# Last phase of a four-layer graph network: reciprocals taken per node, the self term applied while the fourth layer drains, statistics and output by round

## The chip, the cores and the metric

The kernel runs on one core of one Trainium2 chip. The metric is device time in microseconds, the median of several runs; less is better. Engines are named as in the profile: PE multiplies matrices (PEld is its weight load), DVE works elementwise, ACT is ScalarE, POOL is GpSimd, SP issues DMAs.

## What is computed

Node features `x` of 3125 nodes by 64 pass four pre-normalised residual layers over 53125 edges (50000 in both directions and a self loop for each node), which are sorted by destination. The change lies at the end of the fourth:

```python
h = jnp.maximum(_layernorm(x, axis=-1), 0.0)
...
attn = jnp.einsum('ehd,ehd->eh', q[edge_src], k)
amax = jax.ops.segment_max(attn, edge_src, num_segments=n)
ex = jnp.exp(attn - amax[edge_src])
denom = jax.ops.segment_sum(ex, edge_src, num_segments=n)
alpha = ex / (denom[edge_src] + 1e-16)
upd = jax.ops.segment_sum(v * alpha[..., None], edge_src, num_segments=n)
upd = upd.reshape(n, OV) @ W_out
out = tfn_features @ W_self + upd
mu = out.mean(axis=0)
var = out.var(axis=0)
return (out - mu) * jax.lax.rsqrt(var + EPS_BN) * gamma + beta
```

Here `tfn_features` is `h`; there are 8 heads of 16 columns (`OV` = 128), `W_out` is 128 by 64, `W_self` 64 by 64, and the result is added to `x`. Mean and variance run over the nodes, for each of the 64 columns.

## The kernel before

The fourth layer runs over 416 tiles of 128 edges, in groups of four tiles (`GT`), eight groups (`UG`) to a loop iteration, 13 iterations (`NI`), all written out. It is a pipeline of steps: at step (i, k) a group's node rows are transposed, the group before it is multiplied on PE (`products`), the one before that is turned into keys and values on DVE (`keys_and_values`), and so on. `lag(i, k, n)` gives the group that is n steps behind, or nothing. The last stages are `values` (DVE: value rows times softmax weight into the two-deep buffer `M3`), a step later `sums` on PE (per tile one f32 product for the values, L1915, and one bf16 product for the denominators, L1916) in two halves of two tiles, and `add_sums` on DVE, which scales one column of the running sum `acc` (L2087) and adds the tile's sums (L2092). A half of the sums must be there before its adds, and its bank is free again only after them. Every `KG` = 4 groups a softmax step runs through all engines; p1 and p2 in the bodies are its two parts.

After the last group has entered, iteration i == NI has eight more steps, the drain, in which only the later stages have work: no gathers, no `products` but one group, and two halves of softmax. What is in order on an engine there is fixed by the functions `body`, one for each engine.

`acc[:, 0]` then holds, transposed, 128 value columns for each node, and rows 0 to 23 of `acc[:, 1]` hold the denominators, in three parts of 8 heads that must be added. Node n = 25 p + j stands at column n; `node_cols` gives the 125 nodes of one j as a strided view (`NJ` = 25, `PN` = 125). `HT` is `h` transposed, 64 by 3125, column block j for the 125 nodes of j. `rounds(NJ, 4)`, also called `R3`, has six rounds of four blocks (500 columns) and one of one block.

The last phase is a block of its own (L2145 to L2230), behind a barrier of the engines. For each round PE multiplies the 24 rows by `sel_b`, a matrix of zeros and ones that adds the three parts and repeats a head over its 16 columns (L2189; rows 8 to 23 of `sel_b` are copied by two DMAs on SP at the phase's start, L2224); DVE adds 1e-16, takes reciprocals of 128 by 500 and multiplies `acc` in place (L2162, L2163, L2165); PE adds `W_self` and `W_out` products in one bank (L2199, L2200); ACT copies the result to `OT` and adds up its columns (L2214). Then come the mean, one squaring pass over 3125 columns on ACT (L2217), the root (L2219, with a load of its function table), the normalisation of the whole in one DVE instruction (L2176), transposes back on PE (L2206), the add to `X` (L2179) and seven DMAs to the output (L2228).

Of the kernel before, what the change touches and what calls it, by code (L numbers as in the profile page):

```python
# [26 lines left out]
ALU = mybir.AluOpType  # L27
ACT = mybir.ActivationFunctionType
AX = mybir.AxisListType

N = 3125
# [61 lines left out]
def build(nc, A, out):  # L93
    with ExitStack() as ctx:
# [1598 lines left out]
        bcol = sb("bcol", [D, 1])  # L1693
        sel_b = sb("sel_b", [24, 128])
# [45 lines left out]
        fac_cols = bank[7][:, 416:448]  # L1740
        kv_of = lambda k: psum[:, (2 + k % 2 * 2) * 512:(4 + k % 2 * 2) * 512].rearrange("p (t f) -> p t f", t=GT)
# [19 lines left out]
        with nc.Block() as block:  # L1761
            @block.gpsimd
            def _(pool):
                def queries(g):
                    if g >= QR:
                        pool.wait_ge(e3_ev, (g - QR + 1) * 2)
                    for t in range(GT):
# [3 lines left out]
                n = 0  # L1771
                pool.memset(sel_b[0:8, :], 1.0).then_inc(n3_p, 1)
                n += 1
                pool.wait_ge(n3_p, n)

                pool.affine_select(out=sel_b[0:8, :], in_=sel_b[0:8, :], compare_op=ALU.is_ge, fill=0.0, base=0,
                                   pattern=[[1, 128]], channel_multiplier=-16).then_inc(n3_p, 1)
                n += 1
                pool.wait_ge(n3_p, n)
                pool.affine_select(out=sel_b[0:8, :], in_=sel_b[0:8, :], compare_op=ALU.is_ge, fill=0.0, base=15,  # L1780
                                   pattern=[[-1, 128]], channel_multiplier=16).then_inc(n3_p, 1)
# [17 lines left out]
            def _(sp):  # L1799
# [104 lines left out]
            def _(pe):  # L1904
# [34 lines left out]
                def body(i, k):  # L1939
# [9 lines left out]
                    for t in range(GT):  # L1949
# [33 lines left out]

                for r, (j0, n) in enumerate(R3):
# [13 lines left out]
                pe.wait_ge(n3_p, 4)  # L1998
# [4 lines left out]
            def _(dve):  # L2003
# [102 lines left out]
                def body(i, k):  # L2106
# [31 lines left out]
                    if val:  # L2138
                        values(*val)
# [5 lines left out]
        m3_r, m3_b, m3_u, m3_m, m3_c, m3_dve, m3_sd, m3_t, m3_x, m3_o, m3_s = [sem("m3_" + x) for x in  # L2145
            ("r", "b", "u", "m", "c", "dve", "sd", "t", "x", "o", "s")]
        OT = tmp("OT", [D, N])
        OC = tmp("OC", [D, N])
        sq = tmp("sq", [D, N])
        osum = tmp("osum", [D, 8])  # L2150
        rden = tmp("rden", [128, 2, 512])
        bn = tmp("bn", [D, 8])
        CH = rounds(NJ, 4)
        m3_q = sem("m3_q")
        with nc.Block() as block:  # L2155
            @block.vector
            def _(dve):
                c = Chain(dve, m3_r)
                for n, (a, w) in enumerate(CH):
                    dve.wait_ge(m3_b, n + 1)  # L2160
                    r = rden[:, n % 2, 0:w * PN]
                    c.link(dve.tensor_scalar(r, bank[n % 2][:, 0:w * PN], 1e-16, None, ALU.add))  # L2162
                    c.link(dve.reciprocal(r, r))  # L2163
                    v = node_cols(acc[:, 0])[:, a:a + w, :]
                    dve.tensor_tensor(v, v, r.rearrange("c (j p) -> c j p", j=w), ALU.mult).then_inc(m3_u, 1)  # L2165
                dve.wait_ge(m3_c, len(CH))
                c = Chain(dve, m3_dve)
                c.link(dve.tensor_reduce(bn[:, 0:1], osum[:, 0:len(CH)], AX.X, ALU.add))
                c.link(dve.tensor_scalar(bn[:, 1:2], bn[:, 0:1], -1.0 / N, None, ALU.mult))
                c.link(dve.tensor_scalar(OC[:], OT[:], bn[:, 1:2], None, ALU.add))  # L2170
                dve.wait_ge(m3_q, 1)
                c.link(dve.tensor_scalar(bn[:, 3:4], bn[:, 2:3], 1.0 / N, EPS, ALU.mult, ALU.add))
                dve.wait_ge(m3_sd, 1)
                c.link(dve.reciprocal(bn[:, 5:6], bn[:, 4:5]))
                c.link(dve.tensor_tensor(bn[:, 6:7], bn[:, 5:6], gcol[:], ALU.mult))
                c.link(dve.tensor_scalar(OT[:], OC[:], bn[:, 6:7], bcol[:, 0:1], ALU.mult, ALU.add))  # L2176
                for r, (j0, n) in enumerate(rounds(NJ, 4)):
                    dve.wait_ge(m3_t, r + 1)
                    dve.tensor_tensor(X[:, j0:j0 + n, :], X[:, j0:j0 + n, :],  # L2179
                                      bank[4 + r % 2][0:PN, 0:n * D].rearrange("p (j f) -> p j f", j=n), ALU.add).then_inc(m3_x, 1)  # L2180

            @block.tensor
            def _(pe):
                pe.wait_ge(m3_s, 32)
                def denominators(n):
                    a, w = CH[n]
                    if n >= 2:
                        pe.wait_ge(m3_u, n - 1)
                    pe.matmul(bank[n % 2][:, 0:w * PN], sel_b[:], node_cols(acc[0:24, 1])[:, a:a + w, :],  # L2189
                              start=True, stop=True).then_inc(m3_b, 1)  # L2190
                denominators(0)
                for n, (a, w) in enumerate(CH):
                    if n + 1 < len(CH):
                        denominators(n + 1)
# [66 lines left out]
```

## Time and profile before

| | us |
|---|---|
| median of 3 runs | 3128.79 |
| lowest, highest | 3128.04, 3133.41 |
| profiled execution, first to last instruction (span) | 3126.1 |
| fourth layer's drain, last phase (from the timeline) | about 3020 to 3062, 3062 to 3126 |

The profiled execution has no time of its own beside its span; the span is set against the median. In the page, each engine's idle time is put down to what ended it; the chain is followed back from the last instruction, and in this program it reaches back only to the barrier ahead of the last phase. PEclk is TensorE's granted clock as a share of 2.4 GHz: 1.00 or 0.50.

### The profile page before, as it was taken

How to read it: one execution, taken by the hardware profiler on the slowest of the kernel's cores; microseconds unless marked ns; L12 is line 12 of the kernel's file. 1: busy time of each engine (PE TensorE's matmuls, PEld its weight loads, DVE VectorE, ACT ScalarE, POOL GpSimd, SP SyncE). 2: the span in 40 equal slices, each digit the busy share in tenths (PEclk: the TensorE clock that was granted, in tenths of full speed). 3: DMA queues.
4: the chain of work that ended last, by engine and by line, in shares of the span. 5: the costliest groups of instructions: out<-in, count | busy, mean ns of one | idle time of the engine just before them, and what ended most of it. 6: DMA issues, size and time to landing. Idle time of an engine off the chain costs nothing. (4 is left out here: it accounts for less than half of the span.)

```text
span 3126.1 us, 51454 instructions
## 1 busy us (share of the span) xinstructions
PE 2476.7 (79%) x14006; PEld 2130.6 (68%) x14006; DVE 2209.2 (71%) x5060; ACT 864.2 (28%) x2414; POOL 2032.3 (65%) x2119
## 2 busy tenths in 40 slices
PE   5778787525667667477777767999999999999986
PEld 4777787424666666355555556888888888888862
DVE  4555555526888887555555563888888888888875
ACT  1111111136666663111111110222232222323231
POOL 4777777457777771277777736777776677677710
PEclk9776667657888888599999978999999999999985
DMA  3443333133333330155555557889888898888820
GB/s 84 94 89 86 86 87 86 30 68 64 61 60 60 60 52 4 46 155 160 152 160 152 160 147 179 214 206 214 212 206 205 203 216 206 207 204 205 213 68 11
DMA packets 333760, 404.38 MB, mean 129 GB/s; under 512 B 171136, under 2 KB 203006, under 8 KB 333570
## 3 DMA queue, kind: packets, MB, share of 16 engines
q1 hardware_dynamic: 252034, 251.20, 34.4%
q0 software_dynamic: 66560, 96.41, 14.5%
q10 hardware_dynamic: 14976, 54.53, 5.1%
q8 instruction: 84, 1.38, 0.2%
q14 instruction: 106, 0.87, 0.1%
HBM read 339.81 MB, written 62.07 MB: 129 GB/s over the span
## 5 line engine op out<-in xcount | busy, mean ns | idle before, releaser
L1934 PE MATMUL psum<-ckv,z 128*128 128x256 f32 x4160 | 967.8, 383 | 0.0
L1934 PEld LDWEIGHTS psum<-ckv,z 128*128 128x128 f32 x4160 | 766.7, 191 | 97.9
L1768 POOL DMA_INDIRECT acc<-QW,dst_i x416 | 399.5, 960 | 184.6 <-issue 111.2
L234 POOL DMA_INDIRECT ga<-TA,src_i x416 | 412.4, 991 | 161.6 <-issue 126.5
L1789 POOL DMA_INDIRECT ga<-XX,src_i x416 | 399.5, 960 | 162.8 <-issue 122.5
L1027 POOL DMA_INDIRECT ga<-T,src_i x416 | 401.9, 966 | 151.5 <-issue 125.9
L234 POOL DMA_INDIRECT ga<-T,src_i x416 | 396.6, 953 | 149.3 <-issue 124.7
L2048 DVE TENSOR_TENSOR z<-psum,shb 128x2560 f32<-128x2560 f32 x104 | 293.2, 2820 | 66.7 <-PE psum L1925 66.5
L1121 PE MATMUL psum<-HT,wy 128*128 128x128 f32 x1664 | 264.7, 324 | 70.0 <-DVE wy L1394 69.2
L445 PE MATMUL psum<-wre,re 128*128 128x68 f32 x832 | 215.2, 351 | 119.4 <-DVE oneT L290 67.7
L1121 PEld LDWEIGHTS psum<-HT,wy 128*128 128x128 f32 x1664 | 242.8, 232 | 87.8 <-DVE wy L1394 81.5
L445 PEld LDWEIGHTS psum<-wre,re 128*128 128x128 f32 x832 | 174.8, 260 | 140.2 <-issue 137.8
L1668 DVE TENSOR_TENSOR acc<-acc,psum 64x128 f32 x416 | 118.7, 285 | 156.7 <-PE psum L1623 112.3
L1623 PE MATMUL psum<-one,ga 128*128 128x128 f32 x832 | 126.4, 298 | 123.8 <-DMA ga<-T,src_i 114.6
L1623 PEld LDWEIGHTS psum<-one,ga 128*128 128x128 f32 x832 | 109.0, 203 | 158.0 <-issue 147.0
L1607 PEld LDWEIGHTS psum<-w2kv,hid 128*128 128x128 f32 x832 | 161.7, 194 | 70.6 <-issue 52.2
L446 PE MATMUL psum<-win,oneT 128*128 128x64 f32 x832 | 209.1, 344 | 0.0
L2092 DVE TENSOR_TENSOR acc<-acc,psum 128x256 f32 x416 | 175.4, 422 | 38.2 <-PE psum L1916 24.9
L1607 PE MATMUL psum<-w2kv,hid 128*128 128x256 f32 x832 | 199.6, 383 | 0.0
L1636 ACT ACTIVATE hid<-psum,b1kv 128x512 f32<-128x512 f32 x104 | 71.5, 687 | 452.4 <-PE psum L1615 452.4
L1202 DVE TENSOR_TENSOR acc<-acc,psum 128x256 f32 x416 | 173.2, 416 | 26.3 <-DVE acc L1202 8.6
L1656 DVE TENSOR_TENSOR wkvo<-psum,b2kv 128x1024 f32<-128x1024 f32 x104 | 127.4, 1225 | 68.5 <-PE psum L1607 68.3
(362 smaller groups left out, 4142.9 us busy)
## 6 DMA issues: line engine op xcount, KB each, us to landing
shb<-in_ea SPq DMA_DIRECT2D x104, 640.0 KB, 6.2
WKV<-wkvo ACTq DMA_DIRECT2D x104, 512.0 KB
shb<-in_ea SPq DMA_DIRECT2D x104, 512.0 KB, 8.5
wkv<-WKV SPq DMA_DIRECT2D x104, 512.0 KB
dl<-DL SPq DMA_DIRECT2D x208, 128.0 KB
win<-TB SPq DMA_DIRECT2D x416, 32.0 KB
ga<-T,src_i POOLq DMA_INDIRECT x832
ef<-in_ea SPq DMA_DIRECT2D x104, 128.0 KB
```

The lines of the kernel that those rows point to most:

```text
L234: pool.indirect_dma_start(o, None, table, bass.IndirectOffsetOnAxis(ap=src_i[:, g * GT + t:g * GT + t + 1], axis=0)).then_inc(s_g[k], 16)
L445: pe.matmul(P[:, o:o + D + 4], re[:, k % ER, t * W:(t + 1) * W], wre[:], start=True, stop=False)
L446: last = pe.matmul(P[:, o:o + D], oneT[:, k % 2, t * 128:(t + 1) * 128], win[:, k * GT + t, 0:D], start=False, stop=True)
L1027: pool.indirect_dma_start(ga[:, ring(g) + t, :], None, T1, bass.IndirectOffsetOnAxis(ap=src_i[:, g * GT + t:g * GT + t + 1], axis=0)).then ...
L1121: last = pe.matmul(sums_of(n)[:, a * 128:(a + 1) * 128], wy[:, g % YR, t, 2 * a:2 * a + 2, :].rearrange("p h f -> p (h f)"), one[:, g % OR ...
L1607: last = pe.matmul(kvp(k)[:, t * 256:(t + 1) * 256], hid[:, k % 2, t * 128:(t + 1) * 128], w2kv[:], start=True, stop=True)
L1623: last = pe.matmul(bank[k % 2][:, t * 128:(t + 1) * 128], ga[:, pair:pair + 2, :].rearrange("p a f -> p (a f)"), one[:, k * GT + t, :], st ...
L1768: pool.indirect_dma_start(qg[:, (g % QR) * GT + t, :], None, QW, bass.IndirectOffsetOnAxis(ap=dst_i[:, g * GT + t:g * GT + t + 1], axis=0) ...
L1789: pool.indirect_dma_start(ga[:, (g % GR) * GT + t, :], None, XX, bass.IndirectOffsetOnAxis(ap=src_i[:, g * GT + t:g * GT + t + 1], axis=0) ...
L1934: last = pe.matmul(kv_of(k)[:, t, :], z[:, k % 2, j, t * 128:(t + 1) * 128], ckv[:, j, :], start=(j == 0), stop=(j == NZ - 1))
L2048: dve.tensor_tensor(z[:, k % 2], bank[0][:].unsqueeze(1).to_broadcast([128, NZ, GT * W]), shb[:, k % 2], ALU.mult).then_inc(e3_z, 1)
L2092: dve.tensor_tensor(a, a, sums_of(half)[:, (t % 2) * 256:(t % 2 + 1) * 256].rearrange("p (r n) -> p r n", r=2), ALU.add).then_inc(e3_acc, 1)
```

## The change

The parts of the last phase are rewritten, and two pieces move into the drain.

- `own_part`: five of the seven `W_self` products are issued on PE at steps 2, 3 and 4 of the drain, into banks that are free there, and left open; `W_out` adds to them later. Rounds 5 and 6 keep theirs in the last phase.
- In the drain, outside the softmax step p2, DVE runs `values` ahead of `add_sums`, not behind it.
- Denominators: PE transposes the 24 rows of each block to nodes; DVE adds the three parts, adds 1e-16 and takes reciprocals on 125 by 96 and 125 by 104 elements; ACT repeats each 16 times (`recs`), and PE transposes that back to 128 rows. `sel_b` and its two DMAs are gone, as are its three instructions on POOL.
- Statistics: DVE's `bn_stats` per round and one `bn_aggr`, in place of column sums and the squaring pass. A root at the start of ACT's block brings its table load there.
- Normalisation in seven pieces, transposes in a ring of four banks; `beta` is added to `X` by POOL at the phase's start.

```diff
-        bcol = sb("bcol", [D, 1])
-        sel_b = sb("sel_b", [24, 128])
+        brow = sb("brow", [PN, D])
...
+        own_bank = lambda r: bank[(2, 3, 4, 5, 0, 6, 2)[r]]
...
-                    L(bcol[:], A["L3_gnn_beta"].rearrange("a f -> f a"))
+                L(brow[:], A["L3_gnn_beta"].partition_broadcast(PN))
...
+                    if i == NI and 2 <= k <= 4:
+                        pe.wait_ge(e3_ev, NI * UG * 2)
+                        for r in ((0, 1), (2, 3), (4,))[k - 2]:
+                            own_part(r)
...
+                def own_part(r):
+                    j0, n = R3[r]
+                    pe.matmul(own_bank(r)[0:D, 0:n * PN], w_self[:], HT[:, j0 * PN:(j0 + n) * PN], start=True, stop=False)
...
+                    early = i == NI and not p2
+                    if val and early:
+                        values(*val)
...
-                    if val:
+                    if val and not early:
                         values(*val)
...
+                pool.tensor_tensor(X[:], X[:], brow[:].unsqueeze(1).to_broadcast([PN, NJ, D]), ALU.add).then_inc(m3_beta, 1)
...
+                def reciprocals(h):
+                    J, b = DEN[h]
+                    n = J.stop - J.start
+                    dve.wait_ge(m3_den, h + 1)
+                    c.link(dve.tensor_reduce(rec[:, J, :], b[0:PN, 0:n * 24].rearrange("p (j q f) -> p j f q", q=3, f=8), AX.X, ALU.add))
+                    c.link(dve.tensor_scalar(rec[:, J, :], rec[:, J, :], 1e-16, None, ALU.add))
+                    dve.reciprocal(rec[:, J, :], rec[:, J, :]).then_inc(m3_rec, 1)
...
+                def divided(r):
+                    dve.wait_ge(m3_wide, r + 1)
+                    v = nodes_of(acc[:, 0], r)
+                    dve.tensor_tensor(v, v, wide_bank(r)[:, 0:R3[r][1] * PN].rearrange("c (j p) -> c j p", j=R3[r][1]),
+                                      ALU.mult).then_inc(m3_v, 1)
...
+                def statistics(r):
+                    dve.wait_ge(m3_copy, r + 1)
+                    dve.bn_stats(stats[:, r, :], OT[:, cols(r)]).then_inc(m3_stat, 1)
...
+                reciprocals(0)
+                reciprocals(1)
+                for r in range(len(R3)):
+                    divided(r)
+                    if r >= 2:
+                        statistics(r - 2)
+                statistics(LAST - 1)
+                statistics(LAST)
...
+                c.link(dve.bn_aggr(bn[:, 0:2], stats[:].rearrange("p r f -> p (r f)")))
+                c.link(dve.tensor_scalar(bn[:, 2:3], bn[:, 1:2], EPS, None, ALU.add))
                 dve.wait_ge(m3_sd, 1)
...
+                for r in range(len(R3)):
+                    dve.tensor_scalar(OT[:, cols(r)], OT[:, cols(r)], bn[:, 0:1], bn[:, 5:6], ALU.subtract, ALU.mult).then_inc(m3_norm, 1)
+                dve.wait_ge(m3_beta, 1)
...
+                def denominators(h):
+                    J, b = DEN[h]
+                    for j in range(J.start, J.stop):
+                        o = (j - J.start) * 24
+                        last = pe.transpose(b[0:PN, o:o + 24], node_cols(acc[0:24, 1])[:, j, :], ident[0:24, 0:24])
+                    last.then_inc(m3_den, 1)
...
+                def widened(r):
+                    j0, n = R3[r]
+                    pe.wait_ge(m3_rep, r + 1)
+                    if r >= 2:
+                        pe.wait_ge(m3_v, r - 1)
+                    for j in range(n):
+                        last = pe.transpose(wide_bank(r)[:, j * PN:(j + 1) * PN], recs[:, j0 + j, :], ident[0:PN, 0:PN])
+                    last.then_inc(m3_wide, 1)
...
+                    if r >= 5:
+                        pe.matmul(own_bank(r)[0:D, 0:n * PN], w_self[:], HT[:, cols(r)], start=True, stop=False)
+                    pe.matmul(own_bank(r)[0:D, 0:n * PN], w_out[:], nodes_of(acc[:, 0], r), start=False, stop=True).then_inc(m3_out, 1)
...
+                for r, (j0, n) in enumerate(R3):
+                    pe.wait_ge(m3_norm, r + 1)
+                    if r >= 4:
+                        pe.wait_ge(m3_x, r - 3)
...
+                def repeated(r):
+                    j0, n = R3[r]
+                    act.wait_ge(m3_rec, 1 if j0 + n <= DEN[0][0].stop else 2)
+                    act.activation(recs[:, j0:j0 + n, :].rearrange("p j (h c) -> p j h c", h=8),
+                                   rec[:, j0:j0 + n, :].unsqueeze(3).to_broadcast([PN, n, 8, 16]), ACT.Copy).then_inc(m3_rep, 1)
...
+                act.activation(bn[:, 7:8], zero[0:D, 0:1], ACT.Sqrt)
```

The order on PE in the last phase before: a round is a widening product by `sel_b`, then the two output products.

```order
L2189 MATMUL psum<-acc,sel_b 128x500 x2
L2199 MATMUL psum<-HT,w_self 64x500
L2200 MATMUL psum<-acc,w_out 64x500
L2189 MATMUL psum<-acc,sel_b 128x500
L2199 MATMUL psum<-HT,w_self 64x500
```

With the change (L2212 are the denominators' transposes, L2221 the widening ones, L2233 `W_out`):

```order
L2212 MATMUL psum<-ident,acc 125x24 x25
L2221 MATMUL psum<-ident,recs 128x125 x8
L2233 MATMUL psum<-acc,w_out 64x500
L2221 MATMUL psum<-ident,recs 128x125 x4
L2233 MATMUL psum<-acc,w_out 64x500
```

All 25 small transposes now stand first, and a round holds one product of 500 columns where it held three.

On PE in the drain, from the end of step 2 to the start of step 4 with the change (L688, L694 and L701 are the softmax's, L1904 and L1905 the sums', L1979 is `own_part`):

```order
L688 MATMUL psum<-ident,cshift 128x1
L1979 MATMUL psum<-HT,w_self 64x500 x2
L1904 MATMUL psum<-one,edge_a 128x128
...
L694 MATMUL psum<-ident,mx 128x128
...
L701 MATMUL psum<-fdiag,sel 128x16 x2
L1979 MATMUL psum<-HT,w_self 64x500 x2
L1904 MATMUL psum<-one,edge_a 128x128
```

Two `W_self` products stand between step 2's last transpose and step 3's sums, two more between step 3's softmax and step 4's sums; a fifth follows step 4's.

On DVE in the drain, from the end of step 3 into step 4, before (L2075 is `values`):

```order
L730 CAST exb<-exf 128x128
L2075 TENSOR_TENSOR edge_a<-vw,ex 128x512
L264 TENSOR_LOAD base_i
L2087 ISA
L2087 TENSOR_TENSOR acc<-acc,fac 128x2
L2092 TENSOR_TENSOR acc<-acc,psum 128x2x128
```

and with the change (its lines are L2072, L2084, L2089):

```order
L730 CAST exb<-exf 128x128
L2072 TENSOR_TENSOR edge_a<-vw,ex 128x512
L264 TENSOR_LOAD base_i
L2072 TENSOR_TENSOR edge_a<-vw,ex 128x512
L2084 ISA
L2084 TENSOR_TENSOR acc<-acc,fac 128x2
L2089 TENSOR_TENSOR acc<-acc,psum 128x2x128
```

Step 3 keeps its `values` at its end, since it is a softmax step; step 4's now stands ahead of its adds, and those of steps 5 and 6 do the same.

## Rows read from the trace of the kernel before

**Rows 1.** The page's head: the span.

```profile
span 3126.1 us, 51454 instructions
```

**Rows 2.** The chain that ended last, last phase: start us, us, what.

```profile
3062.04 0.06 issue
...
3062.93 1.76 DMA sel_b<-sel_b
...
3072.09 1.92 PE psum L2199 x2
...
3078.08 1.85 PE psum L2199 x2
3079.93 1.98 PE psum L2200 x2
3081.91 2.09 PE psum L2189 x2
...
3105.56 0.64 PE psum L2200 x2
...
3106.97 2.99 ACT sq L2217 x2
...
3109.98 1.28 ACT L2219
...
3111.96 1.91 DVE OT L2176
3113.91 5.31 PE psum L2206 x24
```

**Rows 3.** Stretches: window, length, busy PE, PEld, DVE, ACT, POOL, then PEclk, DMA, GB/s.

```profile
3052.00:3057.00 5.00, 2.82 (x12) 2.26 (x12) 2.80 (x10) 0.00 (x0) 0.00 (x0) 0.50 0.00 0
...
3072.00:3107.00 35.00, 33.45 (x38) 6.48 (x38) 27.15 (x22) 4.43 (x15) 0.00 (x0) 0.50 0.00 0
...
3116.00:3124.00 8.00, 3.42 (x17) 3.23 (x16) 2.13 (x6) 0.00 (x0) 0.00 (x0) 0.50 0.31 100
```

**Rows 4.** Timeline of the drain, PE and DVE: start us, us, instruction, [idle before <-releaser].

```profile
3034.26 0.80 PE L1915 MATMUL psum<-one,edge_a 128*128 128x128 f32 x2 [1.90 <-DVE edge_a L2075]
...
3051.64 0.68 DVE L2075 TENSOR_TENSOR edge_a<-vw,ex 128x512 f32<-128x512 f32 x1
...
3052.38 0.80 PE L1915 MATMUL psum<-one,edge_a 128*128 128x128 f32 x2 [2.22 <-DVE edge_a L2075]
...
3054.03 0.42 DVE L2092 TENSOR_TENSOR acc<-acc,psum 128x256 f32 x1 [1.63 <-PE psum L1916]
...
3056.69 0.68 DVE L2075 TENSOR_TENSOR edge_a<-vw,ex 128x512 f32<-128x512 f32 x1
...
3061.40 0.42 DVE L2092 TENSOR_TENSOR acc<-acc,psum 128x256 f32 x1
```

**Rows 5.** Timeline of PE where the fourth layer begins, the clock at 0.50.

```profile
1840.62 9.95 PE L1988 MATMUL psum<-w2t,acc 128*125 128x64 f32 x40 [4.53 <-PEq L1582]
...
1863.28 1.85 PE L1971 MATMUL psum<-ident,z 125*64 125x125 f32 x8 [8.46 <-DVE z L2031]
```

**Rows 6.** Groups of instructions, shapes apart, whole span: count, busy us, mean ns.

```profile
L2163 DVE RECIPROCAL rden<-rden 128x500 f32<-128x500 f32 x6 | 19.7, 3278 | 0.2
L1244 DVE TENSOR_REDUCE lgt<-psum 128x128 f32<-128x384 f32 x26 | 14.3, 550 | 21.9 <-PE psum L1109 21.8
L2165 DVE TENSOR_TENSOR acc<-acc,rden 128x500 f32<-128x500 f32 x6 | 6.7, 1113 | 0.2
L2162 DVE TENSOR_SCALAR rden<-psum 128x500 f32<-128x500 f32 x6 | 4.1, 677 | 8.4 <-PE psum L2189 8.4
...
L1456 POOL TENSOR_TENSOR X<-X,beta 125x1600 f32<-125x1600 f32 x1 | 3.6, 3592 | 60.6 <-SPq L1444 60.6
...
L1846 ACT ACTIVATE vw<-psum 125x512 f32<-125x512 f32 x6 | 3.6, 598 | 8.9 <-PE psum L1980 8.9
...
L2163 DVE RECIPROCAL rden<-rden 128x125 f32<-128x125 f32 x1 | 0.9, 940 | 0.0
```

**Rows 7.** Timeline of SP's queue at the end: the output's seven DMAs.

```profile
3115.57 4.83 SPq L2228 DMA_DIRECT2D out_x<-X  x7
```

More of the change, by code:

```diff
@@ L2142, in build @@
         layer.close()
-        m3_r, m3_b, m3_u, m3_m, m3_c, m3_dve, m3_sd, m3_t, m3_x, m3_o, m3_s = [sem("m3_" + x) for x in
-            ("r", "b", "u", "m", "c", "dve", "sd", "t", "x", "o", "s")]
+        m3_den, m3_rec, m3_rep, m3_wide, m3_v, m3_out, m3_copy, m3_stat, m3_bn, m3_sd, m3_norm, m3_t, m3_beta, m3_x, m3_o = [sem("m3_" + x) for x in
+            ("den", "rec", "rep", "wide", "v", "out", "copy", "stat", "bn", "sd", "norm", "t", "beta", "x", "o")]
         OT = tmp("OT", [D, N])
-        OC = tmp("OC", [D, N])
@@ L2155, in build, with _ @@
+        nodes_of = lambda v, r: node_cols(v)[:, R3[r][0]:R3[r][0] + R3[r][1], :]
+        LAST = len(R3) - 1
         with nc.Block() as block:
+            @block.gpsimd
+            def _(pool):
+                pool.tensor_tensor(X[:], X[:], brow[:].unsqueeze(1).to_broadcast([PN, NJ, D]), ALU.add).then_inc(m3_beta, 1)
             @block.vector
             def _(dve):
[L2158 to L2165, printed above, removed]
@@ L2174, in _ @@
[L2174 to L2177, printed above, removed]
+                def reciprocals(h):
[5 more added lines that the diff above has]
+                    dve.reciprocal(rec[:, J, :], rec[:, J, :]).then_inc(m3_rec, 1)
@@ L2179, in _ @@
                     dve.tensor_tensor(X[:, j0:j0 + n, :], X[:, j0:j0 + n, :],
-                                      bank[4 + r % 2][0:PN, 0:n * D].rearrange("p (j f) -> p j f", j=n), ALU.add).then_inc(m3_x, 1)
+                                      back_bank(r)[0:PN, 0:n * D].rearrange("p (j f) -> p j f", j=n), ALU.add).then_inc(m3_x, 1)
             @block.tensor
             def _(pe):
[L2184 to L2190, printed above, removed]
@@ L2191, in _ @@
-                denominators(0)
-                for n, (a, w) in enumerate(CH):
-                    if n + 1 < len(CH):
-                        denominators(n + 1)
-                    pe.wait_ge(m3_u, n + 1)
-                    if n >= 2:
-                        pe.wait_ge(m3_c, n - 1)
-                    o = bank[2 + n % 2][0:D, 0:w * PN]
-                    pe.matmul(o, w_self[:], HT[:, a * PN:(a + w) * PN], start=True, stop=False)
-                    pe.matmul(o, w_out[:], node_cols(acc[:, 0])[:, a:a + w, :], start=False, stop=True).then_inc(m3_m, 1)
@@ L2205, in _ @@
+                denominators(0)
+                denominators(1)
+                widened(0)
+                for r in range(len(R3)):
+                    if r < LAST:
+                        widened(r + 1)
+                    outputs(r)
+                for r, (j0, n) in enumerate(R3):
+                    pe.wait_ge(m3_norm, r + 1)
+                    if r >= 4:
+                        pe.wait_ge(m3_x, r - 3)
                     for j in range(n):
-                        last = pe.transpose(bank[4 + r % 2][0:PN, j * D:(j + 1) * D], OT[:, (j0 + j) * PN:(j0 + j + 1) * PN],
+                        last = pe.transpose(back_bank(r)[0:PN, j * D:(j + 1) * D], OT[:, (j0 + j) * PN:(j0 + j + 1) * PN],
```

69 lines of the change are left out of this document (30 added, 39 removed).

## The prediction

> **What bounds it.** I read the page first, then the chain of waits, then the stretches of the end. The span is 3126.1 us [rows 1]; the runs have a median of 3128.8, so 2.7 us lie outside it, and I carry them over unchanged. Nothing in the diff touches the loop of the fourth stage before its last iteration, so only two stretches can move: the drain of that stage, about 3020 to 3062 us, and the last phase, 3062 to 3126, which is a chain from end to end.
>
> In the chain [rows 2] the reader is to see five pieces. The phase begins at 3062.04 with two small DMAs that complete `sel_b`; only then come the sums, their reciprocals, and at 3072.09 the first `w_self` matmul. Then a round repeats every 5.92 us (3078.08 to 3084.00), and in its middle PE alone is on the path: 1.85 for `w_self` (L2199), 1.98 for `w_out` (L2200), 2.09 for the widened denominators (L2189). The last output matmul ends at 3105.56 + 0.64 = 3106.2. Statistics follow until 3111.96 (a squaring pass of 2.99, a table load of 1.28, small operations), a normalisation of 1.91, transposes of 5.31, and the landing of the output. PE is busy 33.45 of 35 us in the rounds, at granted clock 0.50, the 1.2 GHz level [rows 3]: its pace, not DVE's, is the round.
>
> In the drain [rows 4] nothing is full. A step takes 5.05 us (3051.64 to 3056.69): DVE makes the weighted values (0.68, L2075), PE starts 0.06 later, and DVE idles 1.63 until the first half of the sums is there, at 3054.03, then adds. PE is busy 2.82 of 5 us [rows 3]. The two engines wait for each other in turn.
>
> **Drain.** With i == NI and outside the softmax step, `values` now stands ahead of `add_sums`, so PE has its operand a step earlier. From step 5 DVE would run through: four pairs of multiply and add, 2.7 to 3.0 us by [rows 4] (3054.03 to 3056.69 holds them), plus 0.68, about 3.65 us a step in place of 5.05. PE needs 2.82 and is hidden. Three steps (5, 6, 7) gain 1.4, and the move at steps 0 and 1 gains 0.6 out of an idle stretch there. Against this stand five added `w_self` matmuls on PE, in front of the next step's sums. At 1.85 each [rows 2] two of them follow step 2's softmax transposes and end near 3036.1, where step 3's sums began at 3034.3 [rows 4]: with DVE's earlier arrival they cost 1.4 of path. The next two fit under the softmax of step 3 but for 0.2; the fifth delays step 5's first half by 1.2. Laid out step by step from these durations the drain ends near 3059.0 in place of 3061.8 (3061.40 + 0.42): **2.8 us gained**. Bounds: the three steps and the start whole, 4.8 gained; all five on the path, 9.25 less 4.8, so 4.5 lost.
>
> **Entry and rounds.** Let zero be the phase's start. There is no DMA to wait for. PE transposes the 25 blocks of denominators: nearest rows [rows 5] are 40 strided f32 weight loads with 64 moving columns in 9.95, 0.25 each, and the old output transposes, 5.31 for 24 [rows 2], 0.22; I take 0.24, near the first since the stride is the same: 12 by 3.1, all 25 by 6.2. DVE folds the three parts (0.55 for 384 inputs [rows 6], so some 0.45 for 288 or 312), adds (0.68 for 500, so 0.2) and takes reciprocals of 96 and 104 columns; 0.94 for 125 and 3.28 for 500 make that 0.75 and 0.8 [rows 6]. With links 1.5 each: done at 4.6 and, since the second half's transposes end at 6.2, at 7.75. ScalarE's repeated copies of 512 elements cost 0.60 if the broadcast reads like an ordinary copy [rows 6], are ready ahead of PE at round 0, and hide behind PE later; its table load now lies at the phase's start, done long before 4.6. The widening is four transposes with 125 moving columns: 8 such took 1.85 [rows 5], so 0.97 a round with the change of weights. Division stays 1.11 [rows 6], now read from PSUM; the first ends at 8.95.
>
> From 9.0 PE goes on without a gap, since a division (1.11) is shorter than the `w_out` matmul (1.98) beside it: five outputs of 1.98 (9.9), four widenings (3.9), a short one (0.3), round 5 with its `w_self` (1.85 + 1.98 = 3.85), round 6 at a quarter (1.25). That is 19.2, so the last output matmul ends at 28.2. Before it ended at 3106.2 - 3062.04 = 44.2. **16.0 us gained**, nearly all from PE: 2.09 + 1.85 leave a round of 5.92 and 0.97 comes in, and the 10 us of entry shrink to 9.
>
> DVE has the division and a `bn_stats` of 500 per round. No row shows `bn_stats`. The bounds are a fast pass, 1.91 for 3125 (0.31 for 500) [rows 2], and the slowest elementwise operation, the reciprocal, 3.28 for 500 [rows 6]. I take 0.68, the tensor_scalar from PSUM over 500: it too reads every element once and there is no iteration in a sum. Then DVE needs 1.85 a round against PE's 2.95, and it is hidden.
>
> **Statistics.** Before: 3106.2 to 3111.96, 5.76. After: a copy of 125 columns, `bn_stats` of 125, `bn_aggr` over 42 numbers, add, root, reciprocal, product: seven small operations with handovers. By the scaled rows (0.27 for a short PSUM read, about 0.2 for each of the rest, 0.05 a handover) 1.75, between 1.4 and 2.4. The squaring pass, the subtraction and the table load are gone from here. **4.0 us gained.**
>
> **Normalisation to the end.** Before, the start of the normalisation (3111.96) lay 14.14 before the end; the first output DMA left at 3115.57 [rows 7], 3.61 after it, and from there it was 10.5 to the end, with 100 GB/s on the queue through the eight microseconds in which the 0.8 MB moved [rows 3]. I read that as an end set by the transfers, not by the last add. After, DVE first does seven pieces (1.91 x 500/3125 is 0.31, with an instruction's fixed part 0.38), 2.6 together, and only then the first add (0.45): the first DMA leaves 3.05 after the start. PE's transposes hide. With the same 10.5 behind it, **0.6 us gained**; if instead the last add sets the end, 1.5. The added `beta` on POOL, 3.59 us in the same form earlier [rows 6], lies under the rounds; it would cost only beyond 30 us. The removed set-up of `sel_b` on POOL and the swapped load on SP stand under a long wait for the first node table and cost nothing either way.
>
> Sum: 2.8 + 16.0 + 4.0 + 0.6 = 23.4. The profile would then span 3102.7, the median be **3105.4 us**.
>
> **Rivals.**
> *The clock rises.* In rounds of before PE was busy 33.45 of 35 us and stayed at 0.50 [rows 3], so I keep that level. But a third of that time went to 24 rows and a third to 64 rows by 64 columns; now most of it uses 125 or 128 rows, and the drain's gaps are fuller. If PE goes to 2.4 GHz at the third round, the round falls to DVE's 1.85 and five of them gain 5.5: 3100. From the phase's start on it is 10: 3095.5. The Trainium skill, TensorE: Matmul & The Clock Gate, Part 1, says that sustained matmul work releases the throttle; by that rule the rounds of before should have been at full rate, and they were not, so the trace does not bear it out for this kind of work. I give this 0.18.
> *DVE becomes the bound.* If `bn_stats` goes like a reciprocal (3.28), a round costs DVE 4.45, and the last statistics end at 7.8 + 7.5 + 6.3 x 3.28 = 36.0 instead of 28.8: 3112.6. Against it: no row but the reciprocal is that slow. 0.08. **The same mechanism further on is the slower side:** from 2.15 us a call it decides the phase, and from 5.9 us a call (12 ns an element, nearly twice the slowest row) the kernel is slower than before, at 6.9 by over 6 us: 3135. 0.02.
> *The drain gives nothing.* If the five matmuls stay in the way (each in front of sums for which DVE then waits), the drain ends where it did or up to 4.5 later: 3108 to 3113. For it: PE is in order and at half clock. Against it: PE is idle 2.2 of 5 us there [rows 3]. 0.08.
> *It doesn't do what it says.* If the early `values` finds its buffer still in use, or the statistics wait for the last round as before, 1 to 4 us of the gain go, most of it staying: 0.03, near 3108.
>
> **Numbers.** The forecast holds 0.61. A measurement of this kernel tells 0.2%, 6.3 us, from no change. All cases but the slow one stay below 3122.5; I allow 0.02 for a sum of mishaps that leaves less than that. Faster 0.96, same 0.02, slower 0.02. The range runs from 3096, which takes in most of the clock case, to 3113, the upper bound of `bn_stats` at the reciprocal's rate and of the drain.
>
> **What would show it.** Right: the last phase some 43 us long, the first `w_out` matmul about 9 us after its start, a round of about 3 us with PE busy throughout at 0.50; one table load, at the phase's start; about 2 us from the last output matmul to the first normalised piece; DVE's steps 5 to 7 of the drain at about 3.65 us. Wrong: a granted clock of 1.00 in the rounds; DVE idle nowhere in them; `bn_stats` above 2 us; PE waiting for ScalarE's copies; a drain that ends no earlier; an output whose landing stretches as its DMAs leave closer together.

## The result and the profile after

The changed kernel takes 3100.19 us (median of 4 runs, 3097.34 to 3108.21), against 3131.1 for the kernel before in the same comparison: ratio 0.9905, 95% interval 0.9888 to 0.9921. It is faster, and the time lies inside the range, 5.2 below the forecast. The profiled execution took 3097.34; its span, as the page's head below gives it, is 30.5 shorter than that of before [rows 1]. (Of the five runs of phase_only, an experiment below, one took 3420.21 at a granted clock of 0.694; its median and ratio are those of the other four.)

```profile
span 3095.6 us, 51528 instructions
```

Not all of the 30.5 belongs to the change. The timeline of PE at the start of the fourth layer, ahead of any changed instruction (columns: start us, us, instruction, idle before):

```profile
1835.05 9.94 PE L1985 MATMUL psum<-w2t,acc 128*125 128x64 f32 x40 [4.53 <-PEq L1582]
```

Before, the same row begins at 1840.62 [rows 5]: 5.6 us of the difference are there already. So from here on I count from a mark close to the change, DVE's copy L627 with which the softmax of drain step 2 begins, at 3026.65 before and 3020.43 after. Before, it and the same copy one softmax step earlier, ahead of the drain, in DVE's timeline:

```profile
2987.96 0.35 DVE L627 COPY dsth<-dst_f 128x128 f32<-128x128 f32 x1
...
3026.65 0.22 DVE L627 COPY dsth<-dst_f 128x128 f32<-128x128 f32 x1
```

From the mark to the end it was 3126.1 - 3026.65 = 99.5, and is 3095.6 - 3020.43 = 75.2: **24.3 gained**. The gain of the drain's steps 0 and 1 lies ahead of the mark, and it can be read too: from the earlier copy to the mark it was 38.69 and is 38.31 (3020.43 - 2982.12, third fence below), so 0.4 more. Together that is 24.7, where the sum said 23.4.

The chain of waits of the changed kernel, last phase (start us, us, what):

```profile
3054.16 6.01 PE psum L2212 x25
...
3060.96 0.80 DVE rec L2171
3061.76 0.95 DVE acc L2176
...
3062.76 2.05 PE psum L2233 x2
3064.81 1.03 PE psum L2221 x4
3065.84 1.98 PE psum L2233 x2
...
3068.66 1.93 PE psum L2233 x2
3070.60 0.58 PE psum L2221 x4
3071.18 1.94 PE psum L2233 x2
...
3081.68 0.54 DVE OT L2199
```

Against [rows 2]: the two DMAs, the `sel_b` products and the `w_self` products of the first five rounds are gone. The entry is PE's 25 small transposes and the reciprocals of the second half behind them; the first `w_out` stands 8.6 after the start. A round (L2233 to L2233) is 3.08, then 2.82, 2.52, 2.51, where it was 5.92. The shrinking is mostly in the widening (L2221), 1.03 to 0.58, and little in `w_out`, 2.05 to 1.93. The stretches say why (window, length, busy PE, PEld, DVE, ACT, POOL, PEclk, DMA share, GB/s):

```profile
3048.00:3053.00 5.00, 3.72 (x16) 2.54 (x15) 3.80 (x13) 0.00 (x0) 0.00 (x0) 0.50 0.00 0
3054.10:3066.00 11.90, 11.09 (x40) 8.68 (x41) 4.95 (x9) 4.88 (x8) 3.56 (x1) 0.50 0.00 0
3066.00:3070.00 4.00, 4.00 (x8) 0.92 (x7) 2.82 (x4) 1.10 (x2) 0.00 (x0) 0.71 0.00 0
3070.00:3079.70 9.70, 9.70 (x22) 2.12 (x21) 5.04 (x8) 2.52 (x5) 0.00 (x0) 1.00 0.01 2
```

The granted clock rises to 1.00 some 14 us after the phase's start; in before's rounds it stayed at 0.50 [rows 3]. DVE is busy 5.04 of 9.7 there, so it is no bound. In the drain PE is busy 3.72 of 5 us, where it was 2.82 [rows 3], and two things stand against each other (timeline of PE and DVE; its last line is the last output matmul, in the last phase):

```profile
2982.12 0.35 DVE L627 COPY dsth<-dst_f 128x128 f32<-128x128 f32 x1
...
3020.43 0.23 DVE L627 COPY dsth<-dst_f 128x128 f32<-128x128 f32 x1
...
3026.59 3.59 PE L1979 MATMUL psum<-HT,w_self 64*64 64x500 f32 x4
3030.11 0.80 PE L1904 MATMUL psum<-one,edge_a 128*128 128x128 f32 x2
...
3031.76 0.42 DVE L2089 TENSOR_TENSOR acc<-acc,psum 128x256 f32 x1 [1.72 <-PE psum L1905]
...
3040.86 1.93 PE L1979 MATMUL psum<-HT,w_self 64*64 64x500 f32 x2
...
3042.56 0.69 DVE L2072 TENSOR_TENSOR edge_a<-vw,ex 128x512 f32<-128x512 f32 x1
...
3044.37 0.42 DVE L2089 TENSOR_TENSOR acc<-acc,psum 128x256 f32 x1 [1.05 <-PE psum L1905]
...
3047.16 0.69 DVE L2072 TENSOR_TENSOR edge_a<-vw,ex 128x512 f32<-128x512 f32 x1
...
3053.42 0.42 DVE L2089 TENSOR_TENSOR acc<-acc,psum 128x256 f32 x1
...
3079.08 0.64 PE L2233 MATMUL psum<-acc,w_out 128*64 128x125 f32 x2
```

The first pair of `own_part` (3.59 for two) holds step 3's sums until 3030.11, and DVE idles 1.72 for them; the fifth product makes DVE wait 1.05 in step 5, which so takes 4.60 (3042.56 to 3047.16). Then DVE runs through, and the last add begins 32.99 after the mark, where it was 34.75 [rows 4]: 1.8 gained. The division and the operations that no row of before showed, in groups by form over the last phase (count, busy us, mean ns, idle before), then the output's DMAs in SP's timeline:

```profile
L2176 DVE TENSOR_TENSOR acc<-acc,psum 128x500 f32<-128x500 f32 x6 | 6.4, 1093 | 5.1 <-PE psum L2221 5.1
...
L2181 DVE BATCH_NORM_STATS2 stats<-OT 64x6 f32<-64x500 f32 x6 | 4.0, 661 | 2.5 <-ACT OT L2266 2.5
...
L2256 ACT ACTIVATE recs<-rec 125x512 f32<-125x512 f32 x6 | 3.5, 619 | 4.5 <-DVE rec L2171 4.5
```

```profile
3085.07 4.14 SPq L2275 DMA_DIRECT2D out_x<-X  x7
```

The division is what it was [rows 6]. The first output DMA leaves 3.4 after the normalisation began (3081.68), and 10.5 later the span ends, as before, where 3126.1 less 3115.57 [rows 7] was 10.5 too.

### The profile page after: what moved, and what is told of

It reads as the page before. It is cut to its first block and busy times, and to the rows that moved or that the text cites. A ratio compares the mean times of both kernels' runs of the same rounds, so it can differ in the third digit from the quotient of the medians.

```text
span 3095.6 us, 51528 instructions
## 1 busy us (share of the span) xinstructions
PE 2462.2 (80%) x14042; PEld 2124.4 (69%) x14042; DVE 2190.8 (71%) x5063; ACT 863.7 (28%) x2413; POOL 2031.2 (66%) x2117
## 5 line engine op out<-in xcount | busy, mean ns | idle before, releaser
L1121 PE MATMUL psum<-HT,wy 128*128 128x128 f32 x1664 | 266.8, 326 | 63.9 <-DVE wy L1394 63.2
L2089 DVE TENSOR_TENSOR acc<-acc,psum 128x256 f32 x416 | 175.5, 422 | 35.2 <-PE psum L1905 22.0
L407 ACT ACTIVATE msg<-pre 128x256 f32<-128x256 f32 x104 | 43.5, 418 | 476.3 <-DVE pre L500 452.6
```

What stands on the lines that cost most here:

```text
L1121: last = pe.matmul(sums_of(n)[:, a * 128:(a + 1) * 128], wy[:, g % YR, t, 2 * a:2 * a + 2, :].rearrange("p h f -> p (h f)"), one[:, g % OR ...
L2089: dve.tensor_tensor(a, a, sums_of(half)[:, (t % 2) * 256:(t % 2 + 1) * 256].rearrange("p (r n) -> p r n", r=2), ALU.add).then_inc(e3_acc, 1)
```

## The experiments

All but the two repeats are cut from the changed kernel. For each profiled execution I give the drain from the mark (L627) to the first transpose of the last phase (the `sel_b` entry in before), and the last phase from there to the end. "To the mark" is the time from the L627 one softmax step earlier. The two pairs of profiles of one kernel agree in these within 0.3 us, while the start of the fourth layer lies anywhere from 1835.05 to 1847.87 in the twelve profiles; so small effects are read from the stretches, each from one profile, and the median says whether the whole is in keeping. The expectations count the drain to the end of DVE's last add, which is 0.2 to 0.3 less. The ratio is to before, timed in the same comparison.

| kernel | median us | ratio, interval | to the mark | drain | last phase | drain and last phase |
|---|---|---|---|---|---|---|
| before, first profile | 3131.1 | | 38.7 | 35.4 | 64.1 | 99.5 |
| repeat_before | 3128.54 | 1.0002 (0.9993 to 1.0011) | 38.7 | 35.4 | 64.1 | 99.5 |
| the change, first profile | 3100.19 | 0.9905 (0.9888 to 0.9921) | 38.3 | 33.7 | 41.4 | 75.2 |
| repeat_after | 3101.09 | 0.9913 (0.9899 to 0.9926) | 38.3 | 33.7 | 41.2 | 75.0 |
| phase_only | 3118.1 | 0.9966 (0.9951 to 0.9981) | 38.7 | 35.5 | 50.9 | 86.4 |
| early_only | 3105.55 | 0.9933 (0.9915 to 0.9951) | 38.3 | 30.7 | 47.1 | 77.8 |
| own_only | 3108.49 | 0.9935 (0.9918 to 0.9951) | 38.7 | 37.0 | 41.1 | 78.1 |
| contig | 3098.03 | 0.9907 (0.9890 to 0.9923) | 38.3 | 33.8 | 36.4 | 70.1 |
| rows112 | 3101.14 | 0.9911 (0.9894 to 0.9927) | 38.3 | 33.8 | 39.3 | 73.0 |
| interleave | 3102.11 | 0.9917 (0.9900 to 0.9933) | 38.3 | 33.7 | 40.2 | 74.0 |
| own_step1 | 3101.29 | 0.9905 (0.9888 to 0.9922) | 38.3 | 30.9 | 41.1 | 72.0 |
| best | 3092.69 | 0.9876 (0.9859 to 0.9894) | 38.3 | 30.9 | 33.1 | 63.9 |

**Both kernels once more.** No edit.

> The kernel before, once more, for the place of the fourth layer's start. The two profiles so far differ by 30.5 us, but by 5.6 already where PE begins the fourth layer (1840.6 before, 1835.1 after), ahead of any changed instruction. Theory A, that is one execution against another: the start falls between 1834 and 1842 here, with no tie to the kernel. Theory B, the change shifts the first three layers as well (a table in another place, another instruction stream): 1840 to 1841 again, and the last phase 64 us long in either case.

> The changed kernel, once more. Theory A: the fourth layer starts between 1834 and 1842, and the medians of the two repeats differ by 25 (22.6 of last phase and 2.4 of drain). Theory B: the start is at 1835 again, and the medians differ by 30. In both, the last phase is 41.5 us long, and PE's granted clock rises to 1.00 some 14 us into it; if that rise is chance, the phase is 43 to 44 us here.

The start of the layer in the second profile of the kernel before, then of the changed kernel:

```profile
1837.83 9.94 PE L1988 MATMUL psum<-w2t,acc 128*125 128x64 f32 x40 [4.54 <-PEq L1582]
```

```profile
1839.40 9.94 PE L1985 MATMUL psum<-w2t,acc 128*125 128x64 f32 x40 [4.53 <-PEq L1582]
```

They are 1837.8, not 1840 to 1841, and 1839.4, not 1835: the order of the two kernels has turned round, with the same stretches from the mark on. So the 5.6 us ahead of the layer were scatter, and what the change gives is the 24.5 from the mark on in this pair, 24.3 in the first, and the 0.4 ahead of it. The medians alone, 27.8 apart (interval 23 to 32), would not have told the two theories apart. The clock rose again, 13.6 after the phase's start.

**The rewritten phase alone.** `own_part` goes from the drain, every round computes its own product, `values` stands where it stood.

```diff
-                    if i == NI and 2 <= k <= 4:
-                        pe.wait_ge(e3_ev, NI * UG * 2)
-                        for r in ((0, 1), (2, 3), (4,))[k - 2]:
-                            own_part(r)
...
-                    early = i == NI and not p2
+                    early = False
...
-                    if r >= 5:
+                    if r >= 0:
```

> The new last phase alone: the drain as before (values behind the adds, no w_self products on PE), all seven w_self products in the last phase. Theory 1, PE's clock rises in the new rounds because most of their products use 125 or 128 rows: with a product over 64 rows and 64 columns back in each round, as before, it stays at 0.50 and a round is 0.97 + 1.85 + 1.98 = 4.8, so the phase is 41.5 + 5 x 1.85 + 2.6 = 53.4 us. Theory 2, it rises with PE's being busy without gaps: a round falls to 3.5 (0.58 + 0.98 + 1.93), the phase is about 47. The drain from its softmax step (step 2) to its end takes 35.2 again, 1.8 more than with the change.

**The early values alone.** The same without the middle edit.

> As the changed kernel, without w_self products in the drain; values stay ahead of the adds. My reckoning, that the five products delay the drain by 2.8 (1.6 at step 3, 1.2 at step 5): from step 2 to the end the drain takes 33.4 - 2.8 = 30.6. Rival, they are hidden and values alone shapes the drain: 33.4 as with the change. The last phase is as long as in phase_only: 47 or 53. Together 3 to 9 us slower than the changed kernel by my reckoning, 6 to 12 by the rival.

Stretches of the last phase, of the first and of the second kernel:

```profile
3072.50:3092.30 19.80, 19.30 (x32) 5.12 (x32) 6.33 (x8) 3.74 (x8) 0.00 (x0) 0.50 0.00 1
3092.40:3099.00 6.60, 6.60 (x13) 1.23 (x13) 2.69 (x4) 0.97 (x2) 0.00 (x0) 1.00 0.00 0
```

```profile
3066.70:3072.20 5.50, 5.45 (x9) 1.56 (x10) 1.41 (x2) 1.10 (x2) 0.00 (x0) 0.50 0.00 0
3072.20:3086.00 13.80, 13.80 (x31) 2.90 (x29) 6.59 (x10) 3.04 (x6) 0.00 (x0) 1.00 0.00 1
```

The two have the same instructions in the last phase, on all engines, yet in one the clock rises 5.5 us after the first product of 500 columns (14 after the phase's start), in the other 19.4 (28). That is the whole of 50.9 against 47.1. So neither the kind of the phase's products nor PE's running without a gap decides alone when it rises, and neither expected length (53.4 or 47) came out in phase_only. What decides stays open, and with it how much of this stretch's gain is to be counted on: between the two kernels it is 3.8 us. Each has one profile, so that the difference may be one of executions and not of kernels.

The drain falls from 35.5 to 30.7: the early `values` are worth 4.8 there and 0.4 ahead of the mark, when nothing stands in PE's way. That is a little over the prediction's bound, 4.8 for both.

**The early products alone.** Only `early = False`.

> As the changed kernel, with values behind the adds again: the five w_self products alone in the drain. The drain from its softmax step (step 2) to its end was 35.2 before, 30.3 with early values alone, 33.4 with both. My reckoning: the first pair delays step 3's sums by 2.1, the second step 4's by 0.5, the fifth is hidden since step 5's sums now wait for late values: 37.8. Rival, the products fill PE's idle time as the drain of before has it (2.2 of 5 us): 35.2. The last phase is 41.4, so some 4 us slower than the changed kernel, by the rival 2.

The drain takes 37.0, 1.6 more than before's. PE's timeline at step 3:

```profile
3038.45 3.59 PE L1979 MATMUL psum<-HT,w_self 64*64 64x500 f32 x4
3041.97 0.79 PE L1904 MATMUL psum<-one,edge_a 128*128 128x128 f32 x2
```

As in the change, the sums stand right behind the pair. The drain lies nearer the reckoning (37.8) than the rival (35.2). With `values` late the five products cost 1.6, with `values` early 3.1 (33.7 - 30.7): what is late next decides. In the last phase they save 9.8 (50.9 - 41.1), the later rise of the clock in phase_only included. So of the 24.4 the rewritten phase alone gives 13.1 (99.5 - 86.4), and the two pieces in the drain 11.3 more, most of it through the products that need not run in the phase. This split hangs on the clock: with the 47.1 that the same phase took in early_only it would be 16.9 and 7.5.

**What paces a round at the higher clock.** In the change `w_out` took 2.05 at 0.50 and 2.00 at 1.00 in the records, while a `w_self` of as many columns went from 1.93 to 1.05. `w_out` reads `acc` with a stride: nodes of one block stand 25 columns, 100 bytes, apart. This kernel lets the division, which runs anyway, write its result in the order in which PE reads it, into a part of `acc` that is free by then.

```diff
-                    dve.tensor_tensor(v, v, wide_bank(r)[:, 0:R3[r][1] * PN].rearrange("c (j p) -> c j p", j=R3[r][1]),
+                    dve.tensor_tensor(acc[:, 2, cols(r)].rearrange("c (j p) -> c j p", j=R3[r][1]), v, wide_bank(r)[:, 0:R3[r][1] * PN].rearrange("c (j p) -> c j p", j=R3[r][1]),
...
-                    pe.matmul(own_bank(r)[0:D, 0:n * PN], w_out[:], nodes_of(acc[:, 0], r), start=False, stop=True).then_inc(m3_out, 1)
+                    pe.matmul(own_bank(r)[0:D, 0:n * PN], w_out[:], acc[:, 2, cols(r)], start=False, stop=True).then_inc(m3_out, 1)
```

> As the changed kernel, but the division writes its result into a free part of acc with a node round's columns side by side, and w_out reads it there. In the changed kernel a w_out product of 500 columns took 1.98 at granted clock 0.50 and still 1.93 at 1.00, where w_self went from 1.85 to 0.98. Theory, its strided reading sets that pace: now 1.85 at 0.50 and 0.98 at 1.00; from the clock's rise on a round is DVE's 1.75, and the last phase is about 37 in place of 41.4. Rival, the pace comes from 128 rows or from PSUM: 1.93 stays, and 41.4.

PE's timeline, the first round at 0.50 and two later ones at 1.00:

```profile
3069.19 1.93 PE L2233 MATMUL psum<-acc,w_out 128*64 128x500 f32 x2 [0.69 <-DVE acc L2176]
3071.05 1.09 PE L2221 MATMUL psum<-ident,recs 125*128 125x125 f32 x4
...
3073.96 1.05 PE L2233 MATMUL psum<-acc,w_out 128*64 128x500 f32 x2
3074.94 0.65 PE L2221 MATMUL psum<-ident,recs 125*128 125x125 f32 x4
3075.52 1.05 PE L2233 MATMUL psum<-acc,w_out 128*64 128x500 f32 x2
```

And its stretch at 1.00:

```profile
3072.70:3083.00 10.30, 8.37 (x29) 2.72 (x27) 8.34 (x16) 4.10 (x9) 0.00 (x0) 1.00 0.00 0
```

From its start to the next instruction's a `w_out` takes 1.86 at 0.50 and 0.98 at 1.00. A round falls from 2.51 to 1.56, the division stays at 1.04 to 1.09, and the last phase is 5 us shorter: the stride was the pace. DVE is now as busy as PE (8.34 and 8.37 of 10.3), so more from PE would gain little.

**The output's transfers.** Each output DMA is cut into rows 0 to 111 and 112 to 124.

```diff
-                    sp.dma_start(o[:, j0:j0 + n, :], X[:, j0:j0 + n, :]).then_inc(m3_o, 16)
-                sp.wait_ge(m3_o, 16 * len(R3))
+                    for P in (slice(0, 112), slice(112, PN)):
+                        sp.dma_start(o[P, j0:j0 + n, :], X[P, j0:j0 + n, :]).then_inc(m3_o, 16)
+                sp.wait_ge(m3_o, 32 * len(R3))
```

> As the changed kernel, with each of the seven output DMAs cut into one of 112 rows and one of 13. From the first output DMA to the end it was 10.5 in both kernels, the DMA engines' mean share 0.33. Theory, the transfers set the end, and 125 rows go to few of the 16 engines: the share rises towards 0.9, the end falls to the last add plus a landing, 3 us earlier. Rival 1, the pace is that of writing to memory: 10.5 stays. Rival 2, the issue of 14 DMAs on one queue (0.26 to 0.31 each) becomes the end: up to 1 later.

Stretches while only the output moves, of the change and of this kernel, then the output DMAs of both (shortest, median and longest issue in ns, start of the first and of the last):

```profile
3088.00:3093.00 5.00, 0.00 (x0) 0.00 (x0) 0.15 (x2) 0.00 (x0) 0.00 (x0) 0.50 0.34 117
```

```profile
3099.00:3102.00 3.00, 0.00 (x0) 0.00 (x0) 0.00 (x0) 0.00 (x0) 0.00 (x0) 0.50 0.49 139
```

```profile
L2275 SPq DMA_DIRECT2D out_x<-X x7: 263/330/860, 3085.1 to 3088.4; - x7
```

```profile
L2276 SPq DMA_DIRECT2D out_x<-X x14: 340/371/403, 3095.9 to 3101.3; - x14
```

From the first DMA to the end it is 8.4, no longer 10.5. The transfers had set the end, as the prediction had read it, and their shape how long they took. It is the shape and not only the number of DMAs: in the change the last of the seven was issued at 3088.4, and with all of them under way the share stayed at 0.34 to 3093. (A cut at another row was not run.) The gain is 2.1 and the share 0.49, where 3 and 0.9 had been expected, and two stretches of 0.4 us show why:

```profile
3100.70:3101.10 0.40, 0.00 (x0) 0.00 (x0) 0.00 (x0) 0.00 (x0) 0.00 (x0) 0.50 0.38 105
3101.10:3101.50 0.40, 0.00 (x0) 0.00 (x0) 0.00 (x0) 0.00 (x0) 0.00 (x0) 0.50 0.72 215
```

The share swings between these values, as the issues of the 14 DMAs come 0.4 apart on one queue: now the issue is the pace (rival 2's mechanism), and the end stands 3.0 behind the last of them, where in the change it was 7.2. The median shows nothing of 2 us.

**Adds between the normalised pieces.** Instead of seven pieces and then seven adds, DVE takes the add of round r - 2 behind piece r.

```diff
-                for r in range(len(R3)):
+                def normalised(r):
...
+                for r in range(len(R3) + 2):
+                    if r < len(R3):
+                        normalised(r)
+                    if r >= 2:
+                        added(r - 2)
```

> As the changed kernel, with DVE's adds between its normalised pieces (the add of round r behind piece r + 2). The first output DMA then leaves 1.75 after the normalisation's start in place of 3.4. Theory, the transfers set the end: 1.6 us earlier. Rival, the last add does: it comes no earlier, and nothing is gained.

DVE's normalisation and SP's first DMA:

```profile
3091.11 1.43 DVE L2199 TENSOR_SCALAR OT<-OT,bn 64x500 f32<-64x500 f32 x3 [0.17 <-DVE bn L2197]
...
3093.28 4.91 SPq L2282 DMA_DIRECT2D out_x<-X  x7
```

The first DMA leaves 2.2 after the normalisation's start in place of 3.4 (1.75 expected), and the end stands 10.5 behind it, as before, though the last of the seven is issued 0.8 later behind the first (4.91 against 4.14): the last add does not set the end. Worth 1.1, again below what the median tells.

**All five products at the end of drain step 1.** There PE waits for DVE anyway.

```diff
-                    if i == NI and 2 <= k <= 4:
+                    if i == NI and k == 1:
...
-                        for r in ((0, 1), (2, 3), (4,))[k - 2]:
+                        for r in range(5):
```

> As the changed kernel, with all five w_self products at the end of the drain's step 1, where PE stood idle 4.5 to 4.9 us ahead of step 2's softmax transposes, and behind which the granted clock fell to 0.50. Theory, PE kept busy there stays at 1.00: five products of 0.98 fill the gap and delay the transposes by at most 0.5, so the drain from step 2 to its end is 30.3 (early values without the products) or less, against 33.4. Rival, the clock falls anyway: 9.3 us of products in a gap of 4, so the transposes wait 4 to 5 us and the drain ends later than with the change. If the clock is at 1.00 when the last phase begins, that is shorter as well, by up to 4.

PE's product row, then two stretches, of that row and of the drain's end:

```profile
3026.57 4.40 PE L1979 MATMUL psum<-HT,w_self 64*64 64x500 f32 x10 [0.57 <-DVE vw L2060]
```

```profile
3026.60:3031.00 4.40, 4.40 (x11) 1.32 (x12) 3.09 (x11) 0.00 (x0) 0.00 (x0) 1.00 0.00 0
...
3050.30:3053.20 2.90, 1.62 (x12) 1.17 (x12) 2.34 (x8) 1.08 (x4) 0.00 (x0) 1.00 0.00 0
```

All five take 4.4 here, at a clock that is still 1.00, where the change's first two took 3.59; the drain is 30.9, nearly as without the products (30.7). Nor does the mark come later (38.3). So their place had cost 2.9 of the 3.1 us that they add to the drain. The clock has a share in this that no run tells apart: it is still at 1.00 at 3036.2, 6.3 behind the mark, where in the change and in early_only it fell within a microsecond of it, and it is at 1.00 once more for 3 us near the drain's end. By the start of the last phase it has fallen, and that is as long as in the change. The median (3101.29) does not show it. In the profile the fourth layer began at 1843.86, within the scatter named above; with four runs, 3 us do not stand out.

**All of it.** own_step1, contig and interleave, with the 13 last rows of each output piece issued by ACT and the other 112 by SP.

> The changed kernel with own_step1, the contiguous operand of contig, the adds of interleave, and each output DMA cut into 112 rows on SP's queue and 13 on ScalarE's. Theory, the four gains add up (3, 5, 1, and 3 since the second queue takes the issue off the end, where rows112 had 2): the last phase 32 to 33 us, the median 11 to 12 below the changed kernel's, 3089. Rival, they share their end (transfers that start earlier are only paced by the adds, and the clock is as chance has it): 6 to 8 below, 3094.

Output stretch:

```profile
3087.00:3091.50 4.50, 2.79 (x14) 2.60 (x13) 2.57 (x8) 0.00 (x0) 0.00 (x0) 0.50 0.55 158
```

And a stretch near the drain's end, where the instructions are those of own_step1:

```profile
3050.40:3053.30 2.90, 2.33 (x10) 1.86 (x11) 2.33 (x8) 1.08 (x4) 0.00 (x0) 0.50 0.00 0
```

Here the clock stays at 0.50, and in own_step1 it was at 1.00 as far ahead of the last phase: one stream of instructions has seen both levels. The drain is 30.9 with either, so this second rise was worth nothing.

From the mark to the end it takes 63.9, 11.2 less than the change's 75.1; the four pieces by themselves gave 5.0, 2.0, 1.1 and 3.1, also 11.2, so they add up (the fourth piece with the second queue, which was not run by itself; from the first DMA to the end it is 8.1, where rows112 had 8.4). The median is 3092.69, 8.4 below the changed kernel's 3101.09, between the two figures expected; the rest of the 11 lies in stretches that no edit touches, or in the scatter of four runs (the ratio's interval is 11 us wide). It is faster than both kernels: its interval lies below that of repeat_after and overlaps a little that of the change's first comparison, and its slowest run (3095.68) is below the fastest of the change's nine (3097.3).

## Why the prediction was right

**The whole.** 24.4 from the mark on (99.5 to 75.1) and 0.4 ahead of it, so 24.8 against 23.4. The median is 5.2 under the forecast, 4.3 in the second comparison. About 1.4 of it is the sum's error. The rest lies ahead of the drain or in the scatter of the runs: in the second comparison the medians differ by 27.8 with an interval from 23 to 32, which holds 24.8. That the sum came so near is in part luck: its terms missed by -0.7, +2.6, -0.2 and -0.4, and the largest miss is a mechanism that the forecast had kept out of its sum. It is luck as well that the median meets the 3100 of the rival "the clock rises", whose price was wrong.

**Drain, 2.8 forecast.** 2.1: 1.7 from step 2 on and 0.4 in steps 0 and 1, where the forecast had 2.2 and 0.6. Both terms were near: early values 5.2 (4.8 and 0.4), where I had three steps at 1.4 and the start, 4.8 together; five products 3.1, where the working had 1.4, 0.2 and 1.2, 2.8 together. But these terms make 4.8 - 2.8 = 2.0, and not the 2.8 that the prediction states for them: the sum was wrong there, and the terms were better than it. Step 5 took 4.6, since the fifth product stood in the way by 1.05 (forecast 1.2). The rival that the drain gives nothing is out.

**Entry and rounds, 16.0 forecast.** This term was mis-sized: the last output matmul ended 25.6 after the start (3079.72 - 3054.16), so 18.6 were gained. The entry held: transposes 6.0 (6.2), reciprocals done at 4.5 and 7.6 (4.6, 7.75), first `w_out` at 8.6 (9.0). The failing step is that PE "was busy 33.45 of 35 us and stayed at 0.50 [rows 3], so I keep that level". The clock rose, in both profiles of the change and in all eight experiments, and a clock of 1.00 in the rounds stands in the prediction's own list of signs that it is wrong. **Rival "the clock rises", 0.18,** had the mechanism, but its price was wrong: it gave 5.5 from the third round on, on the view that a round falls to DVE's 1.85, and got about 2.2 (the rounds took 17.0 where 19.2 was forecast; the other 0.4 is the entry's), since the strided `w_out` keeps 1.93 at either clock and only the widening and the last two `w_self` products halve. contig shows the rest of that price: with a contiguous operand a round goes down to 1.56, near DVE's pace. The Trainium skill, TensorE: Matmul & The Clock Gate, Part 1, says that sustained matmul work releases the throttle; the changed kernel's rounds agree, the rounds of before (0.50 through 33.45 busy us of 35) and the 28 us of phase_only at 0.50 do not.

**DVE as the bound, and the slower side.** `bn_stats` takes 0.66 for 500 columns; 0.68 was taken from the tensor_scalar row. Both cases are out.

**Statistics, 4.0 forecast:** 1.96 (3079.72 to 3081.68) where it was 5.76, so 3.8. The table load (1.28) lies at the phase's start on an idle ACT, as reckoned.

**Normalisation to the end, 0.6 forecast:** 13.9 where it was 14.1, so 0.2. A piece took 0.43, not 0.38, and the first DMA left 3.4 after the start, not 3.05. The 10.5 behind it held to the tenth.

**Free as reckoned:** ScalarE's copies (0.62) and `beta` on POOL (3.56), which ends 27 us before the first add. The missing `sel_b` set-up lies ahead of the layer, where scatter hides what it is worth.

## What to carry to other kernels

Fill gaps on an in-order engine where it waits for another, and not where its own next product is already due: the same five products cost 3.1 us behind steps 2 to 4 and 0.2 at the end of step 1, where the clock helped too. Before a round is priced at a higher clock, ask of each product whether the clock is what paces it. And when executions scatter by several microseconds ahead of the change, measure from a landmark next to it: that told 1 us apart here where medians could not tell 3.

## What the runs showed of the hardware

- A moving f32 operand with a column stride of 100 bytes held a 500-column product (two instructions) at 1.93 at granted clock 1.00, and 1.98 at 0.50, from its start to the next instruction's; contiguous it took 0.98 and 1.86. The Trainium skill, SBUF — State Buffer, section Door 1: The DMA port swizzle, states that each access that crosses to a new 16-byte line pays a penalty; the runs agree for PE's operand, and show that the price is 0.95 at 1.00 and only 0.12 at 0.50.
- The same instructions of the last phase saw the clock rise 14 us after its start in early_only and 28 in phase_only; in before's phase, with other instructions, it stayed at 0.50 [rows 3]. The same drain saw 3 us at 1.00 in own_step1 and none in best. A rise is no property of a stretch's instructions alone; what else enters stays open.
- Output DMAs of 125 rows kept the DMA engines at a share of 0.34, at 117 GB/s; cut at row 112 it was 0.49 to 0.55, at 139 to 158 GB/s. The Trainium skill, DMA: Bandwidth & Descriptors, section Why a DMA increments its semaphore by 16 and not by 1, says that a transfer is spread over the largest number of engines, up to 16, that divides its slowest dimension on both sides; by that rule an estimate is 5 of 16 engines for 125 rows and 16 for 112. The trace's 0.34 is close to 5 of 16; its 0.49 is a mean over swings between 0.38 and 0.72, while the queue issues one DMA each 0.4 us, and no run here shows the large pieces following each other without such gaps.
